# Moving the transposes of the attention output, and one tile in four of the inner norm to GpSimd

## The reference

```
x = x + attention0(group_norm(x))         # 1024 tokens, 6 heads of 64, relative positions in h and w
t = t + causal_attention(layer_norm(t))   # same tokens, 6 heads of 64, lower triangle only
t = t + ffn(layer_norm(t))                # weights are Kronecker products: 384 -> 1536 -> 384, exact gelu
```

## Time and profile before

| | |
|---|---|
| runs | 2741.86, 2742.15, 2742.36 us |
| profiled execution | 2746.77 us, of which the span from first to last instruction is 2745.0 us |
| busy share of the span | PE 95%, ACT 73%, DVE 69%, POOL 61% |
| chain that ended last, by engine | PE 56%, POOL 17%, DVE 10%, issue 9%, ACT 8% |
| mean granted TensorE clock | 0.984 |

### The profile page before, as it was taken

One profiled execution on the slowest core, in us unless ns is written; L12 is line 12 of the kernel. 1 busy time (PEld: TensorE's weight loads), 2 busy tenths in 40 slices (PEclk: granted clock), 3 DMA queues, 4 the chain that ended last, 5 costly groups with the idle time before them and its releaser, 6 DMA issues.

```text
span 2745.0 us, 69295 instructions
## 1 busy us (share of the span) xinstructions
PE 2597.4 (95%) x29061; PEld 1551.0 (57%) x29061; DVE 1896.2 (69%) x3554; ACT 1995.0 (73%) x2387; POOL 1682.1 (61%) x1152
## 2 busy tenths in 40 slices
PE   7899999999999999999999999999999999999996
PEld 4465655656556564565645656466564665546563
DVE  8775758757676666757677576775767757677574
ACT  6686767868678595785867867678667777678684
POOL 5374666747577375683757737567465665757464
PEclk8899999999999999999999999999999999999998
DMA  3100012000120002100020000300003000110000
GB/s 110 43 2 2 2 30 77 2 1 2 37 69 2 1 2 60 46 2 1 2 82 25 2 1 2 105 2 2 1 8 99 2 2 2 25 59 2 2 1 24
DMA packets 52278, 64.50 MB, mean 23 GB/s; under 512 B 8672, under 2 KB 46176, under 8 KB 51968
## 3 DMA queue, kind: packets, MB, share of 16 engines
q1 hardware_dynamic: 50208, 59.66, 7.2%
q10 hardware_dynamic: 1760, 0.41, 0.1%
HBM read 30.75 MB, written 12.58 MB: 16 GB/s over the span
## 4 chain that ended last, share of the span: by engine, by line
PE 56%; POOL 17%; DVE 10%; issue 9%; ACT 8%; DMA 0%; SPq 0%; POOLq 0%; ACTq 0%; DVEq 0%
POOL pl L1153 16%; PE ps L573 12%; PE ps L1035 9%; PE ps L990 5%; PE ps L1003 5%; PE ps L952 5%; PE ps L804 4%; PE ps L992 4%; PE ps L1244 4%; DVE mxp L1111 3%; DVE qb L748 2%; ACT ph L1066 2%; PE ps L1444 2%; ACT p L1086 2%; PE ps L1465 1%
## 5 line engine op out<-in xcount | busy, mean ns | idle before, releaser
L1153 POOL TENSOR_TENSOR pl<-p,ph 128x1024 f16<-128x1024 f32 (+2 forms) x672 | 1097.6, 1647 | 332.7 <-ACT ph L1066 326.4
L1111 DVE TENSOR_REDUCE mxp<-ps 128x1 f32<-128x512 f32 (+2 forms) x1152 | 700.2, 651 | 196.1 <-PE ps L952 190.5
L1086 ACT ACTIVATE p<-ps 128x1024 f32<-128x1024 f32 (+1 forms) x672 | 639.9, 952 | 137.5 <-PE ps L1003 135.5
L1066 ACT ACTIVATE ph<-p 128x1024 f16<-128x1024 f32 (+1 forms) x672 | 669.3, 996 | 21.4
L1035 PEld LDWEIGHTS ps<-v,ph 128*128 128x128 f16 x9600 | 506.2, 97 | 131.0 <-issue 27.5
L1035 PE MATMUL ps<-v,ph 128*128 128x65 f16 (+1 forms) x9600 | 531.2, 194 | 17.0 <-POOL pl L1153 16.5
L1035 PE MATMUL ps<-v,pl 128*128 128x65 f16 x4800 | 509.4, 193 | 0.0
L1035 PEld LDWEIGHTS ps<-v,pl 128*128 128x128 f16 x4800 | 446.8, 99 | 0.0
L1153 DVE TENSOR_TENSOR pl<-p,ph 128x512 f16<-128x512 f32 (+1 forms) x336 | 257.1, 765 | 183.8 <-ACT ph L1066 182.8
L1003 PE MATMUL ps<-qc,kc 65*128 65x512 f16 (+3 forms) x1344 | 380.3, 364 | 0.0
L822 POOL TENSOR_TENSOR v<-o,v 128x384 f16<-128x384 f32 x128 | 115.6, 920 | 309.9 <-ACT o L818 309.3
(11 more groups left out here) (199 smaller groups left out, 4730.2 us busy)
## 6 DMA issues: line engine op xcount, KB each, us to landing
xin<-in_x SPq DMA_DIRECT2D x8, 1536.0 KB, 6.9
x<-in_x SPq DMA_DIRECT2D x8, 1536.0 KB, 6.8
out<-x SPq DMA_DIRECT2D x16, 768.0 KB, 3.6
qc<-qa SPq DMA_DIRECT2D x42, 128.0 KB
qa<-qa SPq DMA_DIRECT2D x21, 128.0 KB
qb<-qb SPq DMA_DIRECT2D x21, 128.0 KB, 2.3
qa<-o SPq DMA_DIRECT2D x56, 48.0 KB
qb<-o SPq DMA_DIRECT2D x56, 48.0 KB, 2.0
```

The source lines that it names most:

```text
L1066: self.nc.scalar.activation(m.ph[:, i % RING, :, 0:w], m.p32[:, i % RING, :, 0:w], ACT.Copy).then_inc(self.s["hi"], 1)
L1086: nc.scalar.activation(m.p32[:, i % RING, :, 0:w], m.ps[:, 2 * (i % 2):2 * (i % 2) + 2, 0:w], ACT.Exp, scale=SCALE).then_inc(s["exp"], 1)
L1111: nc.vector.reduce_max(to, m.ps[:, bank, 0:w], AX.X).then_inc(s["free"], 1)
L1153: engine.tensor_tensor(m.pl[:, i % RING, part, 0:w], m.p32[:, i % RING, part, 0:w], m.ph[:, i % RING, part, 0:w], ALU.subtract).then_inc(s ...
```

## The change

Four edits.

1. The table of "ot" steps. Layer 0: c = 0 stays at steps 20 and 21, c = 1 moves from 36 and 37 to 38 and 40. Layer 1: c = 0 moves from 16 and 17 to 28 and 30, c = 1 from 28 and 29 to 31 and 33.
2. The order of DVE in the inner norm: `bn_aggr` of tile 3 and `eps` of the first half go ahead of the residual add of tile 4, and `shift` of the first half ahead of `bn_stats` of tile 5.
3. POOL normalises tile 3 and tile 7 (`norm_last`, a new TENSOR_SCALAR instruction on 128 x 384), ACT the other three of each half.
4. At the end of the feed forward the third channel block of `v_products(pe, 0)` goes to the first two, ahead of `ff.down(4)`, and ACT's `v_high(0)` goes ahead of `rel_high` 8 to 11.

```diff
-        for c in range(NC_ - 1):
-            for hf in range(2):
-                steps[(2 * c + 2) * G + LAG + 1 + hf].append(("ot", c, hf))
+        turns = (ends[NH - 1] + 1, ends[NH - 1] + 3, self.N - 5, self.N - 3) if self.causal else (2 * G + LAG + 1, 2 * G + LAG + 2, ends[NH - 1] + 1, ends[NH - 1] + 3)
+        for n, at in enumerate(turns):
+            steps[at].append(("ot", n // 2, n % 2))
...
     def vector(self, dve):
         for t in range(NT):
+            if t == 4:
+                self.aggregate(dve, 3)
+                self.eps(dve, 0)
             self.add(dve, t)
-            if t >= 1:
+            if t >= 1 and t != 4:
                 self.aggregate(dve, t - 1)
-            if t == 4:
-                self.eps(dve, 0)
-            self.statistics(dve, t)
             if t == 5:
                 self.shift(dve, 0)
+            self.statistics(dve, t)
...
+    def norm_last(self, pool, hf, dst):
+
+        t = 4 * hf + 3
+        pool.wait_ge(self.s["shift"], self.s.at("shift", hf + 1))
+        self.nc.gpsimd.tensor_scalar(dst[:, t, :], self.m.x[:, t, :], self.m.ln[:, 1, t:t + 1], self.m.ln[:, 2, t:t + 1],
+                                     ALU.mult, ALU.add).then_inc(self.s["normed_last"], 1)
+
     def gpsimd(self, pool):
         for hf in range(2):
             self.root(pool, hf)
+            self.norm_last(pool, hf, self.m.o)
...
-        for t in range(4):
+        for t in range(3):
             self.proj.norm(act, t, self.m.o)
...
-                    after.v_products(pe, 0, range(NC_ - 1))
+                    after.v_products(pe, 0)
...
-                after.v_products(pe, 0, range(NC_ - 1, NC_))
...
+                w.next.qkv0.v_high(act, 0)
                 for r in range(8, 12):
                     w.next.qkv0.rel_high(act, r)
-                w.next.qkv0.v_high(act, 0)
```

More of the change, by code:

```diff
@@ L1210 @@
     BANKS = (0, 1, 2, 3, 6, 7, 0, 1)
-    COUNTS = dict(biased=8, mm=8, added=8, stats=8, mv=8, eps=2, rstd=2, shift=2, normed=8)
+    COUNTS = dict(biased=8, mm=8, added=8, stats=8, mv=8, eps=2, rstd=2, shift=2, normed=6, normed_last=2)
     def __init__(self, nc, m, layer, s, attn, x_in=None):
@@ L1328, in tensor @@
             for t in range(4 * hf, 4 * hf + 4):
-                pe.wait_ge(self.proj.s["normed"], self.proj.s.at("normed", t + 1))
+                if t % 4 == 3:
+                    pe.wait_ge(self.proj.s["normed_last"], self.proj.s.at("normed_last", hf + 1))
+                else:
+                    pe.wait_ge(self.proj.s["normed"], self.proj.s.at("normed", 3 * hf + t % 4 + 1))
                 mm = self.nc.tensor.transpose(m.ps[:, self.BANKS[hf][c], (t % 4) * P:(t % 4 + 1) * P], m.o[:, t, c * P:(c + 1) * P], m.ident[:, :])
@@ L1341, in scalar @@
             self.high(act, 0, c)
-        for t in range(4, NT):
+        for t in range(4, NT - 1):
             self.proj.norm(act, t, self.m.o)
@@ L1769, in gpsimd @@
             proj0.gpsimd(pool)
-            pool.wait_ge(proj0.s["normed"], proj0.s.at("normed", NT))
+            pool.wait_ge(proj0.s["normed"], proj0.s.at("normed", 6))
+            pool.wait_ge(proj0.s["normed_last"], proj0.s.at("normed_last", 2))
             proj1.bias(pool, slice(0, NT))
```

## The result

The changed kernel takes **2723.32 us** (median of 4 runs, 2721.89 to 2724.88) where the kernel before, beside it, takes 2742.26 us (4 runs, 2741.86 to 2744.44). The ratio is 0.9929, with a 95% interval of 0.9912 to 0.9947: 18.9 us less, where 12.5 less was forecast. The time lies in the range (2721 to 2738), and the direction is the one forecast. But it lies outside the forecast's own range (2725 to 2735), so at least one term was mis-sized.

The account below looks back on a forecast made before the run. In layer 1's attention PE waits for DVE, DVE for ACT, ACT for PE; the inner norm is a chain. Terms -16.3 + 0 + 2.2 + 0 + 1.6 = -12.5 us gave 2734.3 us profiled, 2729.7 us as median; range 2721 to 2738.

Parts of the forecast that it names:

- Layer 1, edit 1: Layer 1's attention: groups 16 to 21 lose 3.01 us, copies return 0.97; net 2.04 an image, 16.3 us in eight.
- Layer 0, edit 1: Layer 0's attention: c = 1 moves between places of equal ACT copy cost; 0, with 0.3 us an image either side.
- Edits 2 and 3: Inner norm: `hT` 0.80 us earlier, but `lT` behind the second shift 0.28 later; loses 0.28 an image, 2.2 us in eight.
- POOL's instruction: Inner norm: POOL's new normalisation takes 1.0 us, bounds 0.7 and 2.0, hidden beside ACT's three tiles; cost 0.
- Edit 4: Seven transitions between images: DVE is late and none of its work moves; 0, between -0.4 and +0.4 us each.
- The clock: Inner norms: falls of PE's granted clock, between 5.3 us less with none and 8.4 more with eight; +1.6 taken.
- Rival (b): Inner norms: the clock falls late in all eight, 8.4 us in place of 1.6, giving 2736.5 us; 17%.
- Rival (a): Inner norm: first half's gain reaches PE, -0.80 in place of +0.28 us an image, 8.6 us less, 2721; 13%.
- Rival (d): Layer 1, behind the last maximum: the four "ot" wait for each other, +5.0 us an image, 2786 us; 4%.

Follow-up runs that it names:

- turns back: The changed kernel with layer 0's four "ot" transposes back at steps 20, 21, 36 and 37: 2729.7 us, ratio 0.9942.
- adjacent: The changed kernel with layer 0's c = 1 transposes at steps 38 and 39 in place of 38 and 40: 2727.35 us in one execution.
- after_again: The changed kernel run once more with no edit, in a later series: 2723.59 us, ratio 0.9927 to the kernel before.
- layer1_turns_only: The kernel before with edit 1 in layer 1 alone: 2730.78 us, ratio 0.9946.
- edit4_only: The kernel before with edit 4 alone: 2744.41 us in one execution, where the kernel before took 2746.56 us.
- dve_order_back: The changed kernel with edit 2 undone (DVE's old order in the inner norm), POOL's normalisation kept: 2719.67 us, ratio 0.9909.
- lows_first: The changed kernel with the inner norm's first two `lT` ahead of the second shift on DVE: 2718.39 us, ratio 0.9897.

## Why the prediction was right, and where it was wrong

- **Layer 1, edit 1: right in mechanism and size.** -16.3 forecast, -14.9 measured, by the alone run. The copies came back at 0.98 (0.97 forecast). The small error is the neighbour: groups 16 to 21 became like 22 to 27 (11.06, the lower bound), not like the mean with 10 to 15.
- **Layer 0, edit 1: wrong, the step that failed most.** The prediction wrote "the order of nothing that waits is changed. I take 0", but PE waited 1.37 us for the bank of "ot" (1, 0), the very wait that the prediction found in layer 1 by the earlier trace rows. It wasn't looked for in layer 0, where the prediction weighed only ACT's copy, and ACT's pace doesn't show it. It costs 0.58 us an image, 4.1 in all, outside the bound of 0.3. This is the largest error of a term that repeats in each image. Two runs (turns back, adjacent) and the last image, which has neither the wait nor the gain, show it.
- **Edits 2 and 3: right for `lT`, wrong in the sum.** +0.28 forecast to the first L573, +0.21 measured. But the account was stopped there. The transposes of the second half used to wait for ACT's fourth tile; with POOL doing that tile at the same time, 0.26 us is won, and nets -0.05 an image: -0.4 in place of +2.2 us.
- **POOL's instruction: 0.66 us in place of 1.0, under the lower bound of 0.7** (called "half", which would have been 0.5). Nothing hung on it, as said: it was hidden.
- **Edit 4: 0 forecast, -0.16 measured,** inside its bound of 0.4. That none of DVE's work is moved looked at the last rows of DVE's chain alone, not at what its first instruction waited for.
- **The clock: +1.6 forecast.** In the profiled pair it was -3.6 us, and a fall after the change cost 1.66 us (1.7 was the bound). From run to run the count varies (below). The medians differ by 18.9 us and the edits' stages make 20.4; the 1.5 us between are near the term of +1.6, but lie inside the interval of the ratio (14.5 to 24.1 us less), so they don't show it right. Rival (b), eight falls, never appeared.
- Rival (a) had 13%: its time (2721) is near the result, its mechanism is not. `lT` stayed behind the shift, and the norm gave 0.05 us an image in place of its 0.80; the missing us came from elsewhere. Rival (d) fell: the "ot" behind the last maximum cost 0.47 or 0.48 us each.

Of the edits -14.1 us were forecast and -20.4 measured. The 6.3 between are 4.1 of layer 0, 2.6 of the norm and 1.0 of edit 4, less 1.4 of layer 1. So the time lies in the range thanks to the one large term; two of the small ones missed in the same direction, and the range was wide enough for them by no merit of the working. The larger miss has one reason: the wait that the change removes was looked for only where the pace of ACT showed it.

## What to carry to other kernels

When a change removes a wait, ask for that wait by name (engine, line, releaser) in every stage that runs the same code: the one in layer 0 cost half a us although ACT's pace didn't show it. Follow a local gain or loss to the next point where the engine runs without a gap, not to the first instruction that moves. And a reordering has its sign from what is late behind it: edit 2 lost 0.21 us an image with the shift ahead of `lT`, and won 0.27 with the shift behind it.

## What the runs showed of the hardware

**GpSimd took two thirds of the time of a TENSOR_TENSOR for a TENSOR_SCALAR.** The TENSOR_SCALAR with two per-row scalars takes 0.66 us on a tile of the size for which a TENSOR_TENSOR takes 0.997 us. The row lists POOL by tile: count, ns min/median/max, first and last start.

```profile
L1315 POOL TENSOR_SCALAR o<-x,ln x16: 661/662/662, 245.5 to 2557.9; 128x384 f32<-128x384 f32 x16
```

The Trainium skill gives about 1.8 cycles an element for a tight loop and 2.6 with two inputs (GPSIMD Engine Reference, "Elementwise — side-by-side cycle accounting"). An estimate from these figures, for 384 elements at the 1.2 GHz that the page gives, is 0.58 and 0.83 us; the ratio of 0.69 is near the measured 0.66, and both measured times are longer than the estimates. Here the two instructions also differ in their operations and in that the second operand of the TENSOR_TENSOR is a broadcast one, so that the count of operands makes the difference is not shown.

**The same kernel had one fall of the clock in one execution and four in another.** PE's timeline of the last norm of the changed kernel shows one fall:

```profile
2558.46 0.61 PE L573 MATMUL ps<-hT,wqkv_hi 128*128 128x512 f16 x1 [1.63 <-DVE lT L1362]
...
2561.42 0.59 PE L573 MATMUL ps<-lT,wqkv_hi 128*128 128x512 f16 x1
2561.85 0.38 PE L573 MATMUL ps<-hT,wqkv_lo 128*128 128x512 f16 x1
```

Seven matmuls take 2.96 us, 0.42 each, where the others start 0.22 apart: that is 1.2 GHz in place of 2.4, behind 1.63 us of waiting. The two profiles of this kernel, with the same stages to 0.02 us where the clock is whole, may come from two chips, but the mean granted clock also differed between the five executions of after_again on one chip (0.986 to 0.989). Of the eight norms, six had a lower clock in the kernel before and four each in layer1_turns_only and edit4_only, which have the norm of before; one and two in the changed kernel, one to four in the four other runs with its norm; none in dve_order_back and in the three with lows_first's order. The wait ahead of the first L573 is 0.68, 1.63, 1.17 and 0.54 us in these four kinds of norm, where the clock is whole. In the kernel before, it isn't even this wait that the fall follows: in the second image the granted clock is 1.00 from 580.40 to 583.00 and 0.50 from 583.20 to 585.00, behind four waits for ACT's tiles (0.89 and three times 0.27 us), and the first L573 comes at 584.96, with no wait. And with 1.63 us it fell in some norms of one execution and not in others with the same waits. So the length of the wait doesn't decide it by itself. The Trainium skill says that the monitor's window is free-running and doesn't reset when a kernel starts (TensorE: Matmul & The Clock Gate, "What's actually happening"). By that rule equal kernels may differ in their falls, and the two executions agree. The two profiled executions of the changed kernel are 3.6 us apart; the stages without a fall, which repeat to 0.02 us between them, are the better measure.
